# A new order for the first stage of a fused attention and memory layer: chunk 0 ahead, normalised rows on ScalarE

## What is computed

```python
mu = jnp.mean(x, axis=-1, keepdims=True)
var = jnp.var(x, axis=-1, keepdims=True)
h = (x - mu) * jax.lax.rsqrt(var + 1e-05) * ln_gamma + ln_beta
qkv = (h @ w_qkv + b_qkv).reshape(B, T, 3, NUM_HEADS, HEAD_DIM)
...
scores = jnp.einsum('bhqd,bhkd->bhqk', q, k) / np.sqrt(HEAD_DIM)
attn = jax.nn.softmax(scores, axis=-1)
out = jnp.einsum('bhqk,bhkd->bhqd', attn, v)
...
out = out @ w_out + b_out
return residual + out
```

## Time and profile before

| | |
|---|---|
| median of 3 runs | 1146.06 us (1140.73 to 1147.0) |
| the profiled execution | 1143.12 us |
| its span in the profile | 1141.0 us |
| PE busy | 1059.6 us (93%) |
| DVE busy | 998.2 us (87%) |
| ACT busy | 808.3 us (71%) |
| POOL busy | 244.1 us (21%) |
| chain that ended last, by engine | PE 73%, DVE 13%, issue 2%, all others 1% or less |

### The profile page before, as it was taken

How to read it: one execution, slowest core, us unless ns; L and a number is a source line. 1 busy time by engine, 2 the same in 40 slices (tenths; PEclk the granted TensorE clock), 3 DMA queues, 4 the chain that set the end, 5 groups by cost and what they waited for, 6 DMA issues and landing times.

```text
span 1141.0 us, 22167 instructions
## 1 busy us (share of the span) xinstructions
PE 1059.6 (93%) x8566; PEld 579.0 (51%) x8566; DVE 998.2 (87%) x1475; ACT 808.3 (71%) x1654; POOL 244.1 (21%) x345
## 2 busy tenths in 40 slices
PE   5897799999999999999999999997899998899995
PEld 4885333333333333333333333334667765788984
DVE  6786999999999999999999999944499998579887
ACT  4462288888888888888888888884567686343443
POOL 5521001101100110100000000102254333565643
PEclk9898599999999999999999999999899998899998
DMA  7595404404413431441342240211134325634321
GB/s 259 163 319 202 56 13 67 66 24 76 68 35 53 68 58 31 76 67 28 60 68 48 41 84 11 93 49 60 47 115 140 114 83 164 198 85 135 103 75 55
DMA packets 87332, 101.55 MB, mean 89 GB/s; under 512 B 21884, under 2 KB 57212, under 8 KB 87228
## 3 DMA queue, kind: packets, MB, share of 16 engines
q1 hardware_dynamic: 86396, 98.56, 35.9%
q10 hardware_dynamic: 832, 1.58, 0.4%
HBM read 55.09 MB, written 43.88 MB: 87 GB/s over the span
## 4 chain that ended last, share of the span: by engine, by line
PE 73%; DVE 13%; issue 2%; POOL 1%; ACT 1%; DMA 1%; SPq 0%; DVEq 0%; PEldq 0%; ACTq 0%; POOLq 0%
PE ps_o L795 26%; PE ps_s L783 20%; PE ps_m L772 10%; PE p_a L1340 3%; DVE maxes L730 2%; PE p_p L1766 2%; DVE p_q_c L1264 1%; DVE p_kv_c L1264 1%; PE p_a L1743 1%; DVE ln_stats L69 1%; PE p_t L1346 1%; PE p_t L1691 1%; PE p_p L1689 1%; DVE p_hid L81 1%; DVE zT_lo L2029 1%
## 5 line engine op out<-in xcount | busy, mean ns | idle before, releaser
L681 ACT ACTIVATE prob<-ps_s 128x512 f32<-128x512 f32 x1024 | 555.7, 597 | 116.8 <-PE ps_s L783 97.3
L730 DVE TENSOR_REDUCE maxes<-ps_m 128x2 f32<-128x1024 f32 x512 | 620.8, 1220 | 18.1 <-PE ps_m L772 13.3
L795 PE MATMUL ps_o<-prob,v_ones 128*32 128x256 f32 x4096 | 327.4, 391 | 7.9 <-issue 6.9
L783 PE MATMUL ps_s<-q_stack,k_stack 64*128 64x512 f32 x1024 | 260.7, 499 | 0.0
L772 PE MATMUL ps_m<-k_stack,q_stack 62*128 62x512 f32 x1024 | 216.8, 416 | 13.3 <-DVE maxes L730 9.7
L783 PEld LDWEIGHTS ps_s<-q_stack,k_stack 64*128 64x128 f32 x1024 | 99.4, 184 | 211.1 <-ACT prob L681 187.6
L795 PEld LDWEIGHTS ps_o<-prob,v_ones 128*32 128x32 f32 x4096 | 81.6, 108 | 195.5 <-ACT prob L681 99.5
L638 POOL COPY v_ones<-v_all 128x512 f32<-128x512 f32 x16 | 9.8, 612 | 528.0 <-PE ps_o L795 528.0
L772 PEld LDWEIGHTS ps_m<-k_stack,q_stack 62*128 62x128 f32 x1024 | 101.5, 192 | 26.6 <-DVE maxes L730 22.7
L405 ACT ACTIVATE p_parts<-ps_qk,cols 128x512 fp32r<-128x512 f32 x32 | 22.0, 687 | 37.8 <-PE ps_qk L450 34.2
L1412 PE MATMUL p_p<-p_hT,w_p 128*128 128x512 f32 x96 | 42.7, 594 | 2.6 <-ACT p_hT L1177 2.6
(11 more groups left out here) (301 smaller groups left out, 1532.1 us busy)
## 6 DMA issues: line engine op xcount, KB each, us to landing
qk_parts<-p_parts SPq DMA_DIRECT2D x32, 512.0 KB, 7.5
q_stack<-qk_parts SPq DMA_DIRECT2D x96, 128.0 KB, 4.7
k_stack<-qk_parts SPq DMA_DIRECT2D x96, 128.0 KB, 7.7
oT<-o_sb SPq DMA_DIRECT2D x32, 256.0 KB, 3.2
x_all<-in_x_dram SPq DMA_DIRECT2D x8, 512.0 KB, 10.3
heads<-oT SPq DMA_DIRECT2D x16, 256.0 KB
inverse<-inverse_sums SPq DMA_DIRECT2D x16, 256.0 KB
out_dram<-x_all SPq DMA_DIRECT2D x7, 512.0 KB, 3.5
```

Of the source, the lines that this page charges most:

```text
L681: act.activation(prob[at % P_RING][:, h], ps_s[:, (GH * at + h) % S_RING], ACT.Exp, scale=HD ** -0.5).then_inc(exp_done, 1)
L730: dve.tensor_reduce(maxes[:, qc, i // 2, i % 2], ps_m[:, i % M_PAIRS], AX.X, ALU.max).then_inc(m_taken, 1)
L783: pe.matmul(ps_s[:, (GH * (UNITS * slot + KT * qc + kt) + h) % S_RING], r32(k_st[slot][rows, pair, kt * P:(kt + 1) * P]), r32(q_st[slot][r ...
L795: ins = pe.matmul(ps_o[32 * h:32 * h + 32, queries], v_st[slot][:, kt, h], prob[(UNITS * slot + KT * qc + kt) % P_RING][:, h, queries], st ...
```

## The change

The diff, cut to its core. `PIECES` is 1, so `clear` clears a whole buffer as before.

```diff
+WARM_UP = 28
...
-        shift, gain = sb("shift", [P, NCH, TPC]), sb("gain", [P, NCH, TPC])
+        shift, gain = sb("shift", [P, NCH, 2, TPC]), sb("gain", [P, NCH, TPC])
...
             for n in range(NCH):
+                if n == 1:
+                    sp.wait_ge(x_in[0], 16)
                 sp.dma_start(x_all[:, tiles(n)], x_c[n]).then_inc(x_in[n], 16)
...
-                pool.tensor_tensor(gain[:, n], rstd[:, n, 0], scalar(const, S_ONE, [P, TPC]), ALU.add).then_inc(sums_ready, 1)
-                steps.did(pool.tensor_tensor(tmp[:, n, 0], mv[:, n, :, 0], rstd[:, n, 0], ALU.mult))
+                mean = mv[:, n, :, 0].unsqueeze(1).to_broadcast([P, 2, TPC])
+                steps.did(pool.tensor_tensor(tmp[:, n], mean, rstd[:, n], ALU.mult))
                 steps.settle()
-                pool.tensor_tensor(shift[:, n], scalar(const, S_ZERO, [P, TPC]), tmp[:, n, 0], ALU.subtract).then_inc(sums_ready, 1)
+                pool.tensor_tensor(shift[:, n], scalar(const, S_ZERO, [P, 2, TPC]), tmp[:, n], ALU.subtract).then_inc(shift_ready, 1)
+                pool.tensor_tensor(gain[:, n], rstd[:, n, 0], scalar(const, S_ONE, [P, TPC]), ALU.add).then_inc(gain_ready, 1)
...
+            clear(stacks["q"][0])
             made.settle()
             deviation(0)
-            deviation(1)
...
+            clear(stacks["k"][0])
+            clear(stacks["q"][1])
+            deviation(1)
+            clear(stacks["k"][1])
+            clear(stacks["q"][2])
             deviation(2)
...
-            clear_stacks(0)
-            deviation(3)
-            clear_stacks(1)
-            clear_stacks(2)
-            for n in range(4, NCH):
+            clear(stacks["k"][2])
+            for n in range(3, NCH):
                 deviation(n)
...
+            widen_beta()
             norm(0)
-            norm(1)
-            put_h(0)
+            put_first_h()
             lower_weights()
             lower_rows(0)
+            norm(1)
+            ternary_size()
             column_bias()
+            row_biases()
             norm(2)
-            put_h(1)
-            ternary_weight()
-            ternary.settle()
             for n in range(NCH):
+                for j in range(4):
+                    left(n, j)
+                if n + 1 < NCH:
+                    lower_rows(n + 1)
                 if n + 3 < NCH:
                     norm(n + 3)
-                left(n, 0)
-                left(n, 1)
-                if n + 2 < NCH:
-                    put_h(n + 2)
-                left(n, 2)
-                left(n, 3)
-                if n + 1 < NCH:
-                    lower_rows(n + 1)
-                if n == 0:
-                    row_biases()
                 values(n)
+                if n == 1:
+                    ternary_weight()
...
             act.dma_start(cols[:], w["cols"]).then_inc(vec_in, 16)
+            act.wait_ge(consts, 2)
+            act.activation(small[:, 4:5], ones[:, 0:1], ACT.Identity)
+            act.wait_ge(x_in[0], 16)
+            act.dma_start(wq, w["w_qkv"].rearrange("(g p) n -> p g n", p=P)).then_inc(wq_in, 16)
             act.dma_start(wt, w["w_ffn"].rearrange("(g p) n -> p g n", p=P)).then_inc(wt_in, 16)
-            act.dma_start(wq, w["w_qkv"].rearrange("(g p) n -> p g n", p=P)).then_inc(wq_in, 16)
...
+            def put_h(n):
+                act.wait_ge(shift_ready, n + 1)
+                if n > 1:
+                    act.wait_ge(hT_turned, n - 1)
+                for i in range(TPC):
+                    ins = act.activation(h[n % 2][:, i], x_all[:, TPC * n + i], ACT.Identity, bias=shift[:, n, 1, i:i + 1], scale=rstd[:, n, 1, i:i + 1])
+                ins.then_inc(h_ready, 1)
...
-            act.wait_ge(wt_in, 16)
-            act.activation(size, wt, ACT.Abs, accum_out=small[:, 0:1]).then_inc(row_sums, 1)
             act.wait_ge(vec_in, 16)
             act.wait_ge(wq_in, 16)
             for c in range(CH):
                 act.activation(r32(wq_hi[:, c]), wq[:, c], ACT.Identity, scale=cols[:, COL_GAMMA + c:COL_GAMMA + c + 1]).then_inc(whi_ready, 1)
+            act.wait_ge(wt_in, 16)
+            act.activation(size, wt, ACT.Abs, accum_out=small[:, 0:1]).then_inc(row_sums, 1)
             turned(0)
             plus_y(0)
+            put_h(1)
             act.wait_ge(col_biased, 1)
             for n in range(NCH):
                 splits(n)
                 if n + 1 < NCH:
                     turned(n + 1)
+                if n + 2 < NCH:
+                    put_h(n + 2)
+                if n + 1 < NCH:
                     plus_y(n + 1)
...
             pe.wait_ge(consts, 12)
+            for i in range(WARM_UP):
+                pe.transpose(ps_t[:, 0, 0:P], const["ident"][:], const["ident"][:])
+            transposes(0)
+            queries_keys(0, range(2))
             pe.wait_ge(row_sums, 1)
-            pe.matmul(ps_v[:, 0, 0, 0:1], ones[:], small[:, 0:1], start=True, stop=True).then_inc(total, 1)
-            transposes(0)
+            pe.matmul(ps_qk[:, 3, 0:1], ones[:], small[:, 0:1], start=True, stop=True).then_inc(total, 1)
             biases()
-            for n in range(NCH):
+            pe.wait_ge(scale_taken, 1)
+            queries_keys(0, range(2, 4))
+            transposes(1)
+            pe.wait_ge(col_biased, 1)
+            pe.wait_ge(row_biased, 1)
+            values(0)
+            for n in range(1, NCH):
                 queries_keys(n)
                 if n + 1 < NCH:
                     transposes(n + 1)
-                if n == 0:
-                    pe.wait_ge(scale_taken, 1)
-                    pe.wait_ge(col_biased, 1)
-                    pe.wait_ge(row_biased, 1)
                 values(n)
```

More of the change, by code:

```diff
@@ L120 @@
 BASES = (0, P // 2)
+PIECES = 1
+WARM_UP = 28
 STACK_LOADS = 16 * 2 * 2 * PAIRS
@@ L183, in project @@
         row_sums, total, scale_taken, ternary_steps = map(sem, ("row_sums", "total", "scale_taken", "ternary_steps"))
-        own, passed, var_ready, rstd_ready, sums_ready = map(sem, ("vector_steps", "passed", "variance", "rstd", "gain_and_shift"))
+        own, passed, var_ready, rstd_ready, gain_ready, shift_ready = map(sem, ("vector_steps", "passed", "variance", "rstd", "gain", "shift"))
         h_ready, hT_turned, hT_ready, x_taken = map(sem, ("h", "hT_in_psum", "hT", "x_plus_y"))
@@ L202, in _ @@
                 if n == 2:
-                    sp.wait_ge(stacks_zeroed, 2 * SLOTS)
+                    sp.wait_ge(stacks_zeroed, 2 * PIECES * SLOTS)
                     for stack in stacks["k"]:
@@ L246, in deviation, with clear @@
                 pool.wait_ge(rstd_ready, n + 1)
-                pool.tensor_tensor(gain[:, n], rstd[:, n, 0], scalar(const, S_ONE, [P, TPC]), ALU.add).then_inc(sums_ready, 1)
-                steps.did(pool.tensor_tensor(tmp[:, n, 0], mv[:, n, :, 0], rstd[:, n, 0], ALU.mult))
+                mean = mv[:, n, :, 0].unsqueeze(1).to_broadcast([P, 2, TPC])
+                steps.did(pool.tensor_tensor(tmp[:, n], mean, rstd[:, n], ALU.mult))
                 steps.settle()
-                pool.tensor_tensor(shift[:, n], scalar(const, S_ZERO, [P, TPC]), tmp[:, n, 0], ALU.subtract).then_inc(sums_ready, 1)
+                pool.tensor_tensor(shift[:, n], scalar(const, S_ZERO, [P, 2, TPC]), tmp[:, n], ALU.subtract).then_inc(shift_ready, 1)
+                pool.tensor_tensor(gain[:, n], rstd[:, n, 0], scalar(const, S_ONE, [P, TPC]), ALU.add).then_inc(gain_ready, 1)
+            def clear(stack):
+                for piece in range(PIECES):
+                    at = slice(piece * (T // PIECES), (piece + 1) * (T // PIECES))
+                    pool.memset(stack[:, :, at], 0.0).then_inc(stacks_zeroed, 1)
+            clear(stacks["q"][0])
             made.settle()
             deviation(0)
-            deviation(1)
             for tile, value in ((const["minus_ident"], 0.0), (i2, 0.0), (const["mean"], 1.0 / HALF), (const["signed_mean"], 1.0 / HALF), (const["ab_init"], 0.0)):
@@ L287, in norm, with put_first_h, widen_beta @@
                 moments(dve, steps, x_all[:, tiles(n)], stats[:, n], mv[:, n], var_ready, passed)
[L289 to L295, removed]
+            def put_first_h():
+                dve.wait_ge(rstd_ready, 1)
+                normalise(dve, x_all[:, tiles(0)], mv[:, 0], rstd[:, 0, 1], h[0], h_ready)
+            def widen_beta():
                 dve.wait_ge(vec_in, 16)
@@ L299, in lower_weights @@
                     dve.tensor_scalar(beta[:, c], ones[:], cols[:, COL_BETA + c:COL_BETA + c + 1], None, ALU.mult).then_inc(beta_ready, 1)
+            def lower_weights():
                 for c in range(CH):
@@ L335, in values, with ternary_size, ternary_weight @@
                     ins.then_inc(v_taken, 1)
-            def ternary_weight():
+            def ternary_size():
                 dve.wait_ge(total, 1)
-                ternary.did(dve.tensor_scalar(small[:, 1:2], ps_v[:, 0, 0, 0:1], 1.0 / (C * C), 1e-5, ALU.mult, ALU.max))
```

(8 more changed lines are left out.)

5 lines of the change are left out of this document (1 added, 4 removed).

## The result

Median 1137.2 us over 12 executions (1133.89 to 1141.73), against 1146.33 for the kernel before on the same chip (12 executions, 1140.73 to 1150.7): a ratio of 0.993, with a 95% interval of 0.9913 to 0.9947. That is 9.1 us by the medians. The forecast was 1135, with a range from 1128 to 1142.

What follows compares the result with a forecast made beforehand. The chain of waits, with PE having most of it, was taken to bound the kernel through the first stage's barrier. The stores' 10.0 us less 0.4 gave 9.6, hence 1133.5 for the profiled execution and 1135 forecast, range 1128 to 1142.

Steps and rivals of the forecast that it cites:

- The sum: First stage: stores' loads begin 10.0 us earlier, less 0.4 for small waits, giving a gain of 9.6 us.
- T: The moment when `hT` of chunk 0 is ready, put at 14.3 us.
- the half share: Loads at the start: the projection weight gets half of 372 GB/s beside x and lands at 10.6 us.
- I take the fast clock at T: Chunk 0 on PE: after warming, the clock stays fast through both waits, so two blocks take 2.78 us.
- rival 1: The clock falls before T: two blocks 5.56 us, biases 4.77, total 1137 to 1139 us; chance 0.20.
- 0.4 for small waits: First stage: 0.4 us taken off the 10.0 us gain, with chunk 4 waiting longer for a store.
- the stores' 10.0: Chunk 1's last piece is there at 34.4 us instead of 44.4, so the loads for the attention begin 10.0 earlier.
- PE's 10.6: Chunk 1 starts at 26.6 instead of 36.99 us, 10.4 gained, plus 0.18 in chunk 1's first block.
- x of chunk 0 alone: First load: x of chunk 0, loaded without others beside it, lands at 4.3 us instead of 5.07.
- the warming: PE before chunk 0: 28 transposes, 6.2 us from about 2 to 8, to have the fast clock at T.
- Rival 2: ACT sets the pace, 0.88 us late in each of chunks 2 to 7: 1140.3 us; chance 0.17 with rival 4.
- Rivals 3 and 4: Weight lands last, 1151.6 us, chance 0.05; stores, not PE, hold the barrier, 1141 us, chance 0.17 together with Rival 2.

Runs made afterwards that it cites:

- r0: The changed kernel run again with no edit; ratio 0.9935 to the kernel before, barrier at 95.85 us.
- r4: The changed kernel with 52 warming transposes instead of 28 and 14 more before chunk 0's first multiplication; barrier at 95.04 us, no ratio.
- r2: The changed kernel without the waits for x of chunk 0, weights issued ahead of ACT's small activation; barrier at 95.50 us, no ratio.
- r3: The changed kernel with the loads of the attention's second group moved behind the barrier; ratio 0.9922 to the kernel before.
- r5: The changed kernel with h of chunks 1 to 7 made on DVE again, in the new order; barrier at 103.34 us, timed once.
- r1: The changed kernel without the 28 warming transposes; chunk 1 starts at 28.08 us, barrier at 97.27 us, no ratio.
- r6: The changed kernel with only its new order: no warming, x and weights issued at once, h on DVE; ratio 0.9997 to the kernel before.
- r8: As r6, but from chunk 1 on DVE does norm and h in their old places; ratio 0.9984 to the kernel before.
- r9: As r6, with the loads of the attention's second group behind the barrier; ratio 0.995 to the kernel before.
- r11: The kernel before with only h of chunks 1 to 7 moved to ACT, old order and loads, no warming; ratio 0.9971.

## Why the prediction was right, and where it was not

Right was the place of the gain. Chunk 1's distance to the steady pace was named as what the change wins, and the barrier as the only way for it to reach the end. The sum said 9.6 and the medians show 9.1 (6.1 to 10.0 by the interval). The small difference hides terms that were off and that the runs show apart, and that they left so little is in part luck.

*The arrivals.* x was put at 4.3 and came at 4.58; the weight at 10.6 and came at 10.54; T at 14.3 and was 13.88. The bytes of the windows and the half share were a good guide here.

*"I take the fast clock at T."* This step failed. The argument was that neither gap was as long as the 5.58 us after which the clock had fallen; it fell with the two of them in the first trace, and within the first alone, of 3.00 us, in r0. The first two blocks took 5.19 us instead of 2.78, r4 measures the price at 1.5 to 2.3, and rival 1, at 0.20, was what happened, though in a milder form than its 1137 to 1139 was worked out from: the biases ran fast, 21.81 - 19.27 = 2.5 us against the 2.7 of the sum, since the clock was back when the blocks had run. The sign that was set for this rival, biases at 333 ns, could not show it: their weight loads took 192. All five traces with the 28 transposes (the first one, r0, r2, r3, r5) run the first multiplications of chunk 0 at half rate. The Trainium skill ("TensorE: Matmul & The Clock Gate", part 1), for which the slow clock is the resting state, agrees with the 0.54 from 12 to 14 us, where PE had next to nothing to do.

*"0.4 for small waits."* For the first trace this term was too small. The prediction saw that the wait of 1.93 (chunk 5's, which it calls chunk 4's) would grow, and left PE out of reach of it; in the first trace it grew to 3.56, reached PE as 1.93 us of idle time and cost another 1.7 at the slow clock (chunk 6's blocks took 84.14 - 76.92 = 7.22 instead of 5.56). In r0 PE idled 0.17 behind it. That spread is not in a sum of single numbers.

*The term that was summed.* The sum took the stores' 10.0, as less than PE's 10.6. Chunk 1 started 1.1 to 1.9 later than 26.6 said, so PE's gain was the smaller one, and it is what arrived: in r0 the last chunk starts at 83.86, 8.9 before the 92.77 of before, and the barrier moved by the same 8.9, 12.0 us behind it in both traces. That 9.6, from the stores less 0.4, comes near is luck.

*x of chunk 0 alone and the warming.* The prediction gave the first a gain of up to 0.87 us in x and T the loss in the weight, without saying which was larger: the loss (r2). It gave the second the fast clock at T, which was not there (r1). Neither part brings anything.

*DVE and ACT.* The prediction counted DVE's relief as 1.35 us less per chunk and gave it no gain. r5, r6 and r8 show that the order needs it to keep what it wins: with chunk 0 shortened, DVE is late with h in chunks 1 to 3. That itself costs 1.9 us in r9 (57.50 from chunk 1 to the last one, where r3 takes 55.58) and 2.4 from chunk 1 to chunk 4 in r6; the wait for stores takes another 1.8 in r6 and more in r5. How much of the lateness is h itself, and how much POOL's clears beside it, is not shown. Rival 2, ACT as the bound, did not come: ACT's 7.67 in a steady chunk of 9.26 hold up nothing, until stores make it wait. Rivals 3 and 4 did not come either: the weight was early, and the barrier followed PE.

## What to carry to other kernels

When a pipeline's first turn is shortened, every engine has to do the first turns' extra work in less time: ask for each of them, not only for the one that paces the steady part, whether it still fits, and which transfers now come due while older ones are still queued ahead of them. A part that frees an engine that is off the critical path can be what lets another part keep its gain, so parts that bring 0 and 3 us alone may bring 8 together. Filling an idle TensorE helped here only where the filling lasted up to the first multiplication that counts. And one trace is not the median: r6 kept 4.6 us at its barrier and nothing over 12 executions.

## What the runs showed of the hardware

Eight transposes between two gaps of 3.72 and 2.25 us did not keep TensorE at 2.4 GHz, while 52 ahead of them and 14 behind them did (r4). In r0 the clock was slow again behind a first gap of 3.00 us. An idle stretch of 2.43 us in r11 left it fast, and one of 1.93 us ahead of the changed kernel's chunk 6 was followed by 3.5 us at half of it: how long the engine idles does not by itself tell whether the clock falls. The granted clock's column showed 1.00 for r1 through blocks that took 4.87 us instead of 2.78: durations are the safer sign early in a trace. The four DVE operations that make h took 1.37 us alone (the kernel before, at 41.54) and 2.41 with one of POOL's clears beside them (r6, at 22.04).
